# A graph layer on one core: the side work of its edge groups set in another order of steps

## The reference, cut to what matters

```python
xn = _layernorm(x)
x = x + gnn(xn) + mix(xn)        # gnn: segment_sum(weight * xn[dst_edge], src_edge) @ W.T + b
# mix: linear attention, then the message and an MLP
#   Q = elu(xn @ Wq) + 1;  K = elu(xn @ Wk) + 1;  KV = K^T (xn @ Wv), over all nodes
#   msg = (Q KV / (Q sum K)) @ Wm;  msg = _layernorm(msg, g1, b1)
#   h = relu(concat([xn, msg]) @ W1) @ W2;  result xn + _layernorm(h, g2, b2)
x = x + moe(_layernorm(x))       # top-2 of 16 experts, silu(h w1) * (h w2) @ w3
```

## Time and profile before

| | us |
|---|---|
| median of 3 runs | 1198.0 (1196.47 to 1198.92) |
| profiled execution | 1197.34 |
| its span, first to last instruction | 1195.6 |
| edge groups 0 to 12 | 106.9 to 737.7 from the span's start |
| one group of 2 to 5 | 47.9 |
| routing and experts | 737.7 to 1195.6 |
| mean granted TensorE clock | 0.963 |

### The profile page before, as it was taken

How to read it: one execution, slowest core, us unless ns; L and a number is a source line. 1 busy time by engine, 2 the same in 40 slices (tenths; PEclk the granted TensorE clock), 3 DMA queues, 4 the chain that set the end, 5 groups by cost and what they waited for, 6 DMA issues and landing times.

```text
span 1195.6 us, 20406 instructions
## 1 busy us (share of the span) xinstructions
PE 1059.3 (89%) x6272; PEld 910.6 (76%) x6272; DVE 774.3 (65%) x1998; ACT 542.8 (45%) x1270; POOL 610.3 (51%) x626
## 2 busy tenths in 40 slices
PE   6897779999999999999999987739999999999980
PEld 5785667787877877878778776229999999999980
DVE  7987688888889888888897768762222222222226
ACT  4444756686776866768758774311001010110100
POOL 5957566767667677676676730012333333333320
PEclk9999899999999999999999998859999999999995
DMA  7314222323223233232232310266999999999948
GB/s 215 106 49 124 71 72 79 92 77 102 85 80 98 84 91 90 77 97 84 87 95 80 102 58 13 96 233 227 333 332 333 324 342 327 337 330 326 341 147 321
DMA packets 113481, 196.03 MB, mean 164 GB/s; under 512 B 13505, under 2 KB 61439, under 8 KB 113407
## 3 DMA queue, kind: packets, MB, share of 16 engines
q1 hardware_dynamic: 84073, 120.62, 30.0%
q0 software_dynamic: 26112, 71.34, 18.9%
q10 hardware_dynamic: 3222, 3.20, 0.8%
HBM read 177.12 MB, written 17.99 MB: 163 GB/s over the span
## 4 chain that ended last, share of the span: by engine, by line
PE 65%; DVE 12%; ACT 12%; DVEq 5%; issue 3%; DMA 2%; ACTq 1%; SPq 0%; POOL 0%; POOLq 0%
PE psum L1114 19%; PE psum L1012 10%; PE psum L1124 9%; PE psum L901 7%; ACT arena L525 6%; PE psum L910 4%; DVE agg L1403 3%; PE psum L790 3%; PE psum L1024 2%; PE psum L891 2%; PE psum L762 2%; ACT hot L425 2%; PE psum L858 2%; DVE agg L1881 2%; DVEq L1462 1%
## 5 line engine op out<-in xcount | busy, mean ns | idle before, releaser
L704 POOL DMA_INDIRECT arena<-y_rows,gather_i x416 | 434.3, 1044 | 208.8 <-PE psum L1024 72.1
L1012 PE MATMUL psum<-arena,hot 128*128 128x256 f32 x832 | 218.6, 395 | 20.7 <-DVE agg L1397 14.7
L1397 DVE TENSOR_TENSOR agg<-psum,agg 128x256 f32 x416 | 174.9, 420 | 48.2 <-DVE agg L1397 26.1
L1012 PEld LDWEIGHTS psum<-arena,hot 128*128 128x128 f32 x832 | 149.8, 194 | 55.4 <-issue 31.7
L638 ACT ACTIVATE arena<-psum 128x512 f32<-128x512 f32 x64 | 38.2, 597 | 327.4 <-PE psum L1114 327.4
L1114 PEld LDWEIGHTS psum<-arena 128*128 128x128 f32 x1536 | 181.2, 194 | 4.9 <-issue 2.5
L1114 PE MATMUL psum<-arena 128*128 128x128 f32 x1536 | 181.6, 277 | 2.0 <-DVE arena L1838 2.0
L1845 DVE TENSOR_TENSOR arena<-psum,arena 128x512 f32<-128x512 f32 x64 | 44.3, 692 | 204.7 <-PE psum L1114 204.7
L720 POOL DMA_INDIRECT chosen_rows<-arena,back_at x64 | 63.2, 987 | 219.8 <-DVE arena L1852 215.1
L525 ACT ACTIVATE arena<-arena,listed 128x256 f32<-128x256 f32 x416 | 171.4, 495 | 0.2 <-DMA arena<-y_rows,gather_i 0.2
L1024 PE MATMUL psum<-arena,first_use 128*128 x624 | 151.8, 386 | 2.9 <-DVE agg L1403 1.8
(11 more groups left out here) (224 smaller groups left out, 1546.9 us busy)
## 6 DMA issues: line engine op xcount, KB each, us to landing
arena<-in_L_ffn_w_dram SPq DMA_DIRECT2D x144, 512.0 KB, 5.7
xnT<-in_L_ffn_w_dram SPq DMA_DIRECT2D x48, 512.0 KB
arena<-y_rows,gather_i POOLq DMA_INDIRECT x416, 2.8
arena<-chosen_rows SPq DMA_DIRECT2D x4, 1280.0 KB, 9.9
y_rows<-w ACTq DMA_DIRECT2D x6, 512.0 KB, 2.9
agg<-in_x_dram SPq DMA_DIRECT2D x4, 640.0 KB, 6.7
n_rows<-arena SPq DMA_DIRECT2D x4, 640.0 KB
out_dram<-agg SPq DMA_DIRECT2D x4, 640.0 KB
```

Source lines behind the costliest of these rows:

```text
L704: pool.indirect_dma_start(rows[h][:, t, :], None, y_rows, bass.IndirectOffsetOnAxis(ap=gather_i[h][:, t:t + 1], axis=0)).then_inc(gathered ...
L1012: pe.matmul(bank_of(g, t // 2)[:, (t % 2) * C:(t % 2 + 1) * C], hot[:, (g * GT + t) % HOTS, :], rows[h][:, t, :], start=True, stop=True).t ...
L1397: dve.tensor_tensor(own, bank_of(g, t // 2)[:, (t % 2) * C:(t % 2 + 1) * C], own, ALU.add).then_inc(evicted, 1)
```

## The change

Only the order of calls in `beside` on PE and DVE and in ACT's loop changes, for groups 1 to 12. No call is added or removed. On PE the message is turned after step 3 in place of 6, `merge` stays at 7, the list is turned at 4 and picked at 6, hidden blocks stand at 21, 22, 26 and 29 in place of 21 (three) and 31, reorders at 24, 31, 36, 37 in place of 26, 27, 32, 35, `query` moves from 28 to 35, `down` from 34 to 35 behind it, `attend` from 39 to 44. The diff, in its core:

```diff
 (ACT)
-                    message_turned(g)
                     if more:
                         keep_list(g + 1)
+                    message_turned(g)
+                    cross_hot(g, 0)
+                    scale_rows(g, 7)
                     std(0, g)
                     first_scaled(g)
                     n1_turned(g)
-                    scale_rows(g, 7)
                     if more:
                         scale_rows(g + 1, 0)
                     hidden_relu(g, 0)
-                    cross_hot(g, 0)
+                    if more:
+                        scale_rows(g + 1, 1)
                     cross_hot(g, 1)
+                    if more:
+                        scale_rows(g + 1, 2)
+                    hidden_relu(g, 1)
+                    cross_hot(g, 2)
                     if more:
                         act.preload_act_table(ACT.Exp)
                         query_exp(g + 1)
                         act.preload_act_table(ACT.Sqrt)
-                    hidden_relu(g, 1)
-                    cross_hot(g, 2)
-                    if more:
-                        scale_rows(g + 1, 1)
+                        own_hot(g + 1, 8)
                     std(1, g)
                     if more:
-                        scale_rows(g + 1, 2)
-                        own_hot(g + 1, 8)
                         scale_rows(g + 1, 3)
...
 (PE, beside)
+                if step == 3:
+                    turn_tok(g, d_msg, d_msgT)
+                if step == 4:
+                    turn_list(g + 1)
                 if step == 6:
-                    turn_tok(g, d_msg, d_msgT)
+                    pick_list(g + 1)
                 if step == 7:
                     merge(g)
...
                 if step == 21:
                     hidden(g, 0)
+                if step == 22:
                     hidden(g, 1)
+                if step == 24:
+                    reorder(g + 2, 0)
+                if step == 26:
                     hidden(g, 2)
+                if step == 29:
+                    hidden(g, 3)
+                if step == 31:
                     reorder(g + 2, 1)
-                if step == 28:
+                if step == 35:
                     query(g + 1)
-                if step == 34:
                     down(g, 0)
                     down(g, 1)
+                if step == 36:
                     reorder(g + 2, 2)
+                if step == 37:
                     reorder(g + 2, 3)
-                if step == 39:
+                if step == 44:
                     attend(g + 1)
...
 (DVE, beside: step before -> step after)
 keep_picked(g + 1)        7 -> 11      keep_places(g + 2)       8 -> 9
 mark_bins(g + 3)         26 -> 13      hot_batch(g + 1, 0)     26 -> 23
 mark_slots(g + 2, 0..3)  14, 19, 24, 29 -> 17, 17, 28, 30
 make_record(g + 2, 0..3) 14, 18, 22, 30 -> 14, 19, 26, 31
 mark_tiles(g + 2, 0..3)  11, 16, 20, 26 -> 11, 16, 24, 29
 pair_stats(1, g)         31, ahead of count_marks -> 33, behind query_elu
 query_elu(g + 1)         30 -> 33      read_parts(g + 2)       33 -> 35
 pair_moments(1, g)       35 -> 37      read_list(g + 2)        37 -> 39
 pair_root, centre(g, 0)  39 -> 41      place_list(g + 2)       41 -> 43
 message_sums(g + 1)      39 -> 43      add_dense(g, 0)         43 -> 47
 mark_starts(g + 2)       55, ahead of message(g + 1, 1) -> behind it
```

More of the change, by code:

```diff
@@ L987, in beside @@
                         down(g, 1)
-                if step == 35:
+                if step == 36:
+                    if sorts:
+                        reorder(g + 2, 2)
+                if step == 37:
                     if sorts:
                         reorder(g + 2, 3)
-                if step == 39:
+                if step == 44:
                     if more:
@@ L1583, in beside @@
                     pair_moments(0, g)
-                    if more:
-                        keep_picked(g + 1)
                 if step == 8:
-                    if sorts:
-                        keep_places(g + 2)
                     hot_batch(g, 16)
@@ L1591, in beside @@
                     first_root(g)
+                    if sorts:
+                        keep_places(g + 2)
                 if step == 11:
+                    if more:
+                        keep_picked(g + 1)
                     if sorts:
                         mark_tiles(g + 2, 0)
+                if step == 13:
+                    if counts:
+                        mark_bins(g + 3)
                 if step == 14:
@@ L1597, in beside @@
                         make_record(g + 2, 0)
-                    if sorts:
-                        mark_slots(g + 2, 0)
                 if step == 15:
@@ L1604, in beside @@
                         mark_tiles(g + 2, 1)
-                if step == 18:
+                if step == 17:
+                    if sorts:
+                        mark_slots(g + 2, 0)
+                    if sorts:
+                        mark_slots(g + 2, 1)
+                if step == 19:
                     if sorts:
                         make_record(g + 2, 1)
[L1608 to L1611, removed]
+                if step == 23:
+                    if more:
+                        hot_batch(g + 1, 0)
+                if step == 24:
                     if sorts:
                         mark_tiles(g + 2, 2)
-                if step == 22:
+                if step == 26:
                     if sorts:
                         make_record(g + 2, 2)
-                if step == 24:
+                if step == 28:
                     if sorts:
                         mark_slots(g + 2, 2)
-                if step == 26:
-                    if counts:
-                        mark_bins(g + 3)
+                if step == 29:
                     if sorts:
                         mark_tiles(g + 2, 3)
-                    if more:
-                        hot_batch(g + 1, 0)
-                if step == 29:
+                if step == 30:
                     if sorts:
                         mark_slots(g + 2, 3)
-                if step == 30:
-                    if more:
-                        query_elu(g + 1)
+                if step == 31:
                     if sorts:
                         make_record(g + 2, 3)
-                if step == 31:
-                    pair_stats(1, g, d_down, 4)
                     if counts:
@@ L1639, in beside @@
                 if step == 33:
+                    if more:
+                        query_elu(g + 1)
+                    pair_stats(1, g, d_down, 4)
+                if step == 35:
                     if sorts:
                         read_parts(g + 2)
-                if step == 35:
+                if step == 37:
                     pair_moments(1, g)
-                if step == 37:
+                if step == 39:
                     if sorts:
                         read_list(g + 2)
-                if step == 39:
+                if step == 41:
                     pair_root(1, g)
                     centre(g, 0)
+                if step == 43:
+                    if sorts:
+                        place_list(g + 2)
                     if more:
                         message_sums(g + 1)
[L1652 to L1656, removed]
                 if step == 45:
@@ L1659, in beside @@
                 if step == 47:
+                    add_dense(g, 0, step)
                     if more:
@@ L1672, in beside @@
                 if step == 55:
+                    if more:
+                        message(g + 1, 1)
                     if sorts:
                         mark_starts(g + 2)
-                    if more:
-                        message(g + 1, 1)
             def add_up(g, its_bin):
```

9 lines of the change are left out of this document (1 added, 8 removed).

## The result

| | before | after |
|---|---|---|
| median of 4 runs | 1197.95 us (1196.47 to 1198.92) | 1177.21 us (1175.21 to 1177.64) |
| ratio, 95% interval | | 0.9823 (0.9811 to 0.9835) |
| profiled execution, span | 1197.34, 1195.6 | 1175.21, 1173.4 |

The kernel after is 1.8% faster: 20.7 us by the medians, 22.1 by the two profiled executions (the one after lies 2.0 under its median, the one before 0.6 under). The forecast was 1178.4, in a range of 1170 to 1190.

The account below looks back on a forecast made before the run. Each group was bound by a DVE half and a PE half in turn; 1.6 us saved in each of groups 2 to 10 (14.4), plus 1.2, 2.8 and 1.2 in groups 1, 11, 12: 19.6 off 1198.0 gives 1178.4, range 1170 to 1190.

Parts of the forecast that it names:

- DVE half: Stretch from the end of `down` to own tile 16, 24.33 us before; 2.6 out, 0.9 in, 1.7 shorter.
- PE half: Stretch from own tile 16 to the end of `down`, 23.60 us before; net +0.1, including tile 20 waiting some 0.3.
- Scan out: On VectorE the scan runs before the wait for `down` instead of behind the statistics, taking out 1.76 us a group.
- Pair out: On VectorE the first pair eviction also runs before the wait for `down`, taking out 0.60 us a group.
- D: The end of `down` in a group, the point where the PE half ends and the DVE half begins.
- Waits put in: New VectorE waits behind `down`: 0.7 us before the list's first read, 0.2 before pair 6; sum 0.9.
- `keep_places` and `keep_picked`: Two small VectorE operations leave the path to tile 9's eviction, 0.10 us net each; bounds of both 0 and 0.2.
- The merge's chain: Message turn and copies before PE's merge: copy done 4.7 us into the group, merge wanted at 5.3; PE's moves count 0.
- ACT's order: Relu 1 to exponential's end 6.7 us, 1.0 to spare; rival: ACT comes late, kernel slower, 1208, chance 0.08.
- GpSimd: Gathers in the GpSimd queue cost 0, bounds 0 and 1 us; one wait near 5 across `query` and `down`.
- "no gain" rival: GpSimd queue or message copy sets the pace, groups back at 47 to 48, kernel 1196 to 1200 us; chance 0.06.
- merge and ring waits: In group 11, some 1.1 us of waits go, beside 1.7 of `down` waiting for relu 1; 2.8 in all.

Follow-up runs that it names:

- e1: Kernel before with the scan and the statistics of VectorE's step 31 swapped, scan first; 1196.53 us, ratio 0.9991.
- f1: Kernel before with the statistics moved from step 31 to 32, behind scan and register load but ahead of the first pair eviction; 1180.00 us, ratio 0.9851.
- b1: Kernel before with the statistics alone moved from step 31 to 33, behind the first pair eviction, and pair_moments from 35 to 37; 1180.96 us, ratio 0.9857.
- a2: Kernel after with PE's early turns of message and list and ACT's copies put back in their old places; 1175.85 us, ratio 0.9814.
- a3: Kernel after with `query` put back from step 35 to 28; 1180.15 us, ratio 0.9850.
- c1: Kernel after with `query` moved behind `down` and the last reorder, and `attend`, `query_elu`, message steps and ACT's order adapted; 1192.83 us, ratio 0.9958.
- f2: Kernel after with the register load `bins_named` moved from step 31 to 33, behind `query_elu` and the statistics; 1184.42 us, ratio 0.9887.

## Why the prediction was right

The time, the sign and the group (46.3 forecast, 46.32 measured) came out, in part by luck: the largest term, the scan, held only because the change also moved a register load that the sum did not have. Going by the steps:

- *DVE half, 1.7 shorter*: 24.33 went to 12.10 + 10.76 = 22.86, 1.5 shorter. *PE half, 0.1 longer*: it is 0.14 shorter, so tile 20's wait of 0.3 never came. The two misses of 0.2 cancel.
- *Scan out, 1.76*: the amount held, the reason was half of it. The sum left out the register load behind the scan, which the trace of before has under its own line. Had the change put the statistics behind the scan alone, the same sum would have given the same 1180, and e1 shows 1196.5. That the change moved the statistics past the load as well is what made the step right, and that was luck. I had looked at busy rows alone, and a sequencer's work is in none of them; I had also taken groups 2 to 10 as alike, where group 10 of the trace before has no scan and is as long.
- *Pair out, 0.60*: f1 keeps it in and is as fast as b1, with D to the next start at 10.58 for both. What the pair gains is spent at the new waits (0.69 before the list's read). It did not count by itself.
- *Waits put in, 0.9*: the list's read 0.69 (0.7) and pair 6 0.17 (0.2), which starts 0.09 behind the end of the operation ahead of it (357.09) where others start 0.08 before it. DVE's wait for `down` is 1.00 (near 1), D to the next start 10.76 (10.7). f1 needs 10.58 there because one reorder (0.58) stands ahead of D and a cross tile (0.43) behind it instead; its PE half is 0.15 longer for it (23.61 beside 23.46). The prediction's "8 tiles at 0.216 x 2" for the reorder's price are four tiles, eight matmuls; the 0.6 is right all the same.
- *`keep_places` and `keep_picked`, 0.2*: half of it came. From tile 8's eviction to the one-hots it was 0.44 (331.12 to 331.56) and is 0.34 (324.89 to 325.23). `keep_picked` stood between two evictions that are no closer without it: 0.63 apart with it (330.49, 331.12), 0.64 without (324.25, 324.89).
- *The merge's chain, 0*: no ACT wait, the copy done at 4.6 us into the group (4.7), and a2 shows that all of it is worth nothing.
- *ACT's order*: 6.66 from relu 1 to the exponential's end (6.7), 1.00 to spare (1.0). But the gate that cost a3 its time is another, the second root behind the own one-hots; the prediction gave no slack for it.
- *GpSimd, 0*: right in cost, wrong in its picture. Its one wait is 2.26, not near 5, because gathers took longer than 0.95: 1.90, 1.64 and 2.43 in group 4, begun 0.13 to 0.39 after the start of an own one-hot or the scan on DVE (346.43 beside 346.29). The rule that the prediction weighed, of the port pair in the Trainium skill, "SBUF — State Buffer", section "SBUF: two separate sides", would have them do so; the trace agrees. But the last gather before that wait was done at 350.11, 2.26 before the next began, so the "no gain" rival had no hold. No run moved the gathers alone. One sign that the prediction gave for being wrong did appear: ACT's scalings wait for gathers, 30.5 us in 13 waits over the whole kernel, where it was 0.2 us before. It cost groups 2 to 10 nothing, since the scaling ends 2.2 us into the group (317.11), where the prediction had it (2).
- *Group by group*: for groups 2 to 10, 14.4 was forecast and 14.9 came (groups 9 and 10 stayed at 47.0, groups 6 and 7 lost more than 1.6). Group 1 gave 2.0 (1.2), group 12 0.8 (1.2), and group 11 4.1 (2.8). In group 11 the wait of `down` for relu 1, 1.7, went as forecast (tile 16 to D from 22.50 to 20.93); the step that was short is the rest, "some 1.1 of its merge and ring waits", which measured 2.5: 1.4 before tile 16, and 1.1 behind D, where before there was a ring wait of 0.6 and the register load stood bare. b1 and f1, with the old order of PE and ACT, keep the 22.50. Together the groups gave 21.8 in the profiled executions, where 19.6 was forecast; by the medians the gain is 20.7. Waits of PE in group 11, after: us in total, times, longest.

```profile
PE psum L1014 <- DVE agg L1399: 0.6, 1, 0.6
PE psum L883 <- ACT wv L433: 0.2, 1, 0.2
```

So the gain of 20.7 has two parts: 17 to 18 by statistics moved past scan and load (b1, f1), and some 3 by all other moves together, in groups 11, 1 and 12. Within groups 2 to 10 the other moves give nothing (418.2 in all three).

That groups 9 and 10 take 0.7 more than the others lies in the groups before them. `add_dense` puts a `dve.drain()` on either side of its addition where the pair eviction of that step meets the same node tiles; at steps 47 and 49 that is so for both additions of groups 8 and 9 and for no other group (`meets_pair`, L1476 after). In group 8 the second addition starts 10.01 behind D where in group 3 it starts 9.49, and tile 0's eviction in the group after comes 0.79 later. With the first addition at its old step 43 (before, b1, f1) other groups are the long ones: 46.6 to 47.0 in groups 7 to 10 of f1, against 46.3 in its groups 2 to 6. No run moved the additions alone, so this is read from code and rows, not shown.

Left open: what of group 1's 2.0 is due to its stretch at a granted clock of 0.93.

## What to carry to other kernels

Between two engines that meet once in a cycle, split the cycle there and price each move in its half; but ask for every place whether the engine really runs ahead of the other at that point (c1: free after the group's start, 3.3 us behind `down`). An idle time whose named releaser was done long ago is a sign of work that busy time doesn't count: ask for the sequencer's rows by line before moving anything past them. When several moves come together, try the one that takes work out from behind a wait alone in the old kernel: here it was one call and over four fifths of the gain.

## What the runs showed of the hardware

- Loading 32 registers from SBUF kept DVE's sequencer 2.10 us (before: 13 times, 2098 to 2353 ns). In e1 and f2 the instruction behind it started 0.12 after its end, though all that it needed was there; placed behind a waiting instruction it starts only when that does (357.14 beside 357.12 before, 357.85 beside 357.83 in e1, 351.63 beside 351.62 in f2). Where nothing ahead of it waits it starts before the operations in front of it have run: at 345.0 after, ahead of the record and the scan of 346.29.
- A gather's issue took 0.94 to 0.97 us, with one exception of 1.07, unless it began while DVE ran an operation on two SBUF inputs (one-hots, the sort's fp16 compares and records, the scan, the sums of the dense rows). Then it ended 0.82 after that operation's end, 0.75 after the scan's, where this is later than 0.94 from its own start: 346.43 + 2.43 = 348.86 beside 346.29 + 1.82 = 348.11 above. Between 150 and 700 us all 203 gathers after (164 before) that began beside no DVE operation or beside an eviction alone took at most 0.96. A long operation of one input, the reduction of 1.55, stretched none of 13. One begun before the operation, or no more than 0.02 after its start (325.25 beside the one-hots of 325.23: 0.95), wasn't touched.
